# Another table of issue places for the delta rule's steps on TensorE, VectorE and ScalarE

## The reference

```python
S = S * gt[..., None]
pred = jnp.einsum('bhk,bhkv->bhv', kt, S)
delta = (vt - pred) * bt[..., None]
S = S + kt[..., None] * delta[:, :, None, :]
o = jnp.einsum('bhk,bhkv->bhv', qt, S)
```

## Time and profile before

| what | value |
| --- | --- |
| runs | 1614.93, 1616.38, 1616.94 us; median 1616.38 |
| the profiled execution's own time | 1616.59 us |
| its span, first to last instruction | 1614.8 us |
| mean granted TensorE clock | 0.964 |
| busy: TensorE, VectorE, ScalarE | 1409.9, 1199.5, 1019.0 us |
| ScalarE's instructions | 2716 |

### The profile page before, as it was taken

One profiled execution on the slowest core, in us unless ns is written; L12 is line 12 of the kernel. 1 busy time (PEld: TensorE's weight loads), 2 busy tenths in 40 slices (PEclk: granted clock), 3 DMA queues, 4 the chain that ended last, 5 costly groups with the idle time before them and its releaser, 6 DMA issues. The chain is left out here.

```text
span 1614.8 us, 41750 instructions
## 1 busy us (share of the span) xinstructions
PE 1409.9 (87%) x15104; PEld 937.5 (58%) x15104; DVE 1199.5 (74%) x3775; ACT 1019.0 (63%) x2716; POOL 41.2 (3%) x49
## 2 busy tenths in 40 slices
PE   6888889978999878888988989988989889988888
PEld 2544555656455446556756756665666667566634
DVE  6848888974842487898888889898888988974221
ACT  5617888995611456777777777686777767754220
POOL 0000000000000000000000000000000000000000
PEclk9989899989999997999999999999999999979999
DMA  4025001000030011122121212212121211200010
GB/s 168 0 83 128 15 15 28 2 2 1 1 134 0 28 31 49 20 62 56 23 66 52 69 20 63 61 31 52 58 63 19 69 55 23 51 25 15 0 55 26
DMA packets 128489, 69.30 MB, mean 43 GB/s; under 512 B 104464, under 2 KB 115984, under 8 KB 127264
## 3 DMA queue, kind: packets, MB, share of 16 engines
q1 hardware_dynamic: 128288, 66.64, 15.3%
HBM read 51.36 MB, written 6.98 MB: 36 GB/s over the span
## 5 line engine op out<-in xcount | busy, mean ns | idle before, releaser
L1666 DVE SCALAR_TENSOR_TENSOR arena<-arena 128x1024 f32<-128x1024 f32 x144 | 183.0, 1280 | 19.6 <-ACT arena L1235 19.3
L882 PE MATMUL bank<-xt,arena 128*128 128x512 f32 x384 | 183.1, 608 | 9.6 <-ACT arena L1227 8.2
L1745 DVE TENSOR_TENSOR arena<-arena 128x512 f32<-128x512 f32 x224 | 155.2, 693 | 9.5 <-PE bank L938 4.5
L716 PE MATMUL bank<-xt,arena 128*128 128x512 f32 x320 | 142.2, 601 | 3.8 <-DVE arena L1478 3.8
L1234 ACT COPY arena<-bank 128x512 f32<-128x512 f32 x96 | 56.2, 585 | 92.4 <-PE bank L882 90.8
L882 PEld LDWEIGHTS bank<-xt,arena 128*128 128x128 f32 x384 | 68.4, 194 | 71.9 <-issue 71.6
L716 PEld LDWEIGHTS bank<-xt,arena 128*128 128x128 f32 x320 | 60.3, 192 | 85.3 <-issue 85.1
L735 PE MATMUL bank<-arena 128*128 128x256 f32 (+2 forms) x384 | 98.4, 404 | 6.2 <-DVE arena L1478 5.3
L938 PEld LDWEIGHTS bank<-arena 128*32 128x32 f32 x5120 | 59.8, 115 | 75.5 <-issue 64.4
L1164 ACT ACTIVATE arena<-arena 128x128 f32<-128x128 f32 x256 | 99.5, 393 | 0.0
L938 PE MATMUL bank<-arena 128*32 128x32 f32 x5120 | 74.7, 204 | 25.8 <-DVE arena L1747 17.3
(11 more groups left out here) (170 smaller groups left out, 3313.3 us busy)
## 6 DMA issues: line engine op xcount, KB each, us to landing
arena<-d_w SPq DMA_DIRECT2D x16, 519.0 KB, 6.4
arena<-beta_scratch SPq DMA_DIRECT2D x16, 512.0 KB, 5.7
arena<-zero_scratch SPq DMA_DIRECT2D x14, 512.0 KB, 4.6
arena<-arena SPq DMA_DIRECT2D x64, 64.0 KB, 2.6
arena<-zero_scratch SPq DMA_DIRECT2D x15, 256.0 KB, 2.9
arena<-arena SPq DMA_DIRECT2D x12, 256.0 KB, 3.8
arena<-w_scratch SPq DMA_DIRECT2D x2, 1376.0 KB, 6.1
arena<-f_idx SPq DMA_DIRECT2D x2, 1072.0 KB, 8.4
```

Of the source, the lines that this page charges most:

```text
L716: last = pe.matmul(bank[2 * w + n % 2][0:rows, :], (WU if f < 2 else WU1R)[:, w, k, m * P:m * P + rows], XT[:, k, hf * HALF:(hf + 1) * HAL ...
L882: last = pe.matmul(bank[b][:], DW[:, par, c:c + P], XT[:, k, rhs], start=(k == 0), stop=(k == KC - 1))
L1666: dve.scalar_tensor_tensor(out=CT[:, x], in0=RAW[:, x, 3 - j:3 - j + S], scalar=DW[:, par, tap:tap + 1], in1=CT[:, x], op0=ALU.mult, op1=A ...
L1745: dve.tensor_tensor(kq, kq, left, ALU.mult)
```

## The change

It replaces the numbers of the three tables `"pe"`, `"act"` and `"dve"` of `PLACE`. The steps are the same, and so is all other code. Many numbers move without changing the order. In the diff, a step's neighbours tell whether it did.

```diff
--- before.py
+++ after.py
@@ -61,56 +61,56 @@
 
 PLACE = {
     "pe": [
-        (0.226, "piece", 7), (0.432, "piece", 2), (0.486, "piece", 3), (0.582, "piece", 1), (0.596, "piece", 0),
-        (0.692, "piece", 6), (0.733, "piece", 4), (0.774, "piece", 5), (0.966, "norm", 0), (0.993, "norm", 1),
-        (1.267, "level", 0, 1), (1.281, "level", 0, 0), (1.322, "turn_v", 1), (1.363, "level", 1, 1), (1.39, "level", 1, 0),
-        (1.445, "level", 2, 1), (1.459, "level", 2, 0), (1.5, "level", 3, 1), (1.514, "level", 3, 0), (1.541, "norm_q"),
-        (1.555, "level", 4, 0), (1.637, "level", 5, 0), (1.664, "turn_v", 0), (1.705, "level", 4, 1), (1.842, "level", 5, 1),
-        (1.856, "level", 6, 0), (1.884, "gate", 0), (1.938, "level", 6, 1), (1.952, "gate", 1), (2.021, "left", 4, 0),
-        (2.034, "left", 4, 1), (2.062, "right", 4, 0), (2.116, "right", 4, 1), (2.13, "left", 5, 0), (2.144, "left", 5, 1),
-        (2.185, "right", 5, 0), (2.212, "keys", 0), (2.24, "right", 5, 1), (2.253, "left", 6, 0), (2.295, "right", 6, 0),
-        (2.308, "left", 6, 1), (2.336, "keys", 1), (2.349, "solve", 0), (2.377, "right", 6, 1), (2.404, "update", 0),
-        (2.473, "predict", 1), (2.527, "solve", 1), (2.568, "update", 1), (2.61, "predict", 2), (2.623, "solve", 2),
-        (2.651, "update", 2), (2.719, "predict", 3), (2.747, "solve", 3), (2.76, "update", 3), (2.788, "predict", 4),
-        (2.801, "solve", 4), (2.829, "update", 4), (2.87, "predict", 5), (2.897, "solve", 5), (2.925, "update", 5),
-        (2.979, "predict", 6), (3.007, "solve", 6), (3.048, "update", 6), (3.075, "predict", 7), (3.103, "solve", 7),
-        (3.158, "update", 7), (3.199, "final"), (3.418, "turn_out", 0), (3.678, "turn_out", 1), (3.815, "project", 0),
-        (3.911, "project", 1), (4.089, "project", 2), (4.171, "project", 3),
+        (0.212, "piece", 7), (0.445, "piece", 2), (0.486, "piece", 3), (0.568, "piece", 1), (0.61, "piece", 0),
+        (0.692, "piece", 6), (0.747, "piece", 4), (0.788, "piece", 5), (0.979, "norm", 0), (1.007, "norm", 1),
+        (1.281, "level", 0, 1), (1.295, "level", 0, 0), (1.336, "turn_v", 1), (1.377, "level", 1, 1), (1.404, "level", 1, 0),
+        (1.459, "level", 2, 1), (1.473, "level", 2, 0), (1.514, "level", 3, 1), (1.527, "level", 3, 0), (1.555, "norm_q"),
+        (1.582, "level", 4, 0), (1.651, "level", 5, 0), (1.678, "turn_v", 0), (1.719, "level", 4, 1), (1.856, "level", 5, 1),
+        (1.87, "level", 6, 0), (1.897, "gate", 0), (1.938, "level", 6, 1), (1.966, "gate", 1), (2.034, "left", 4, 0),
+        (2.062, "left", 4, 1), (2.075, "right", 4, 0), (2.13, "right", 4, 1), (2.144, "left", 5, 0), (2.158, "left", 5, 1),
+        (2.199, "right", 5, 0), (2.24, "left", 6, 0), (2.253, "right", 5, 1), (2.267, "keys", 0), (2.308, "right", 6, 0),
+        (2.322, "left", 6, 1), (2.349, "solve", 0), (2.363, "keys", 1), (2.39, "right", 6, 1), (2.418, "update", 0),
+        (2.5, "predict", 1), (2.541, "solve", 1), (2.596, "update", 1), (2.623, "predict", 2), (2.637, "solve", 2),
+        (2.664, "update", 2), (2.733, "predict", 3), (2.76, "solve", 3), (2.774, "update", 3), (2.801, "predict", 4),
+        (2.815, "solve", 4), (2.842, "update", 4), (2.884, "predict", 5), (2.925, "solve", 5), (2.952, "update", 5),
+        (2.993, "predict", 6), (3.021, "solve", 6), (3.048, "update", 6), (3.089, "predict", 7), (3.116, "solve", 7),
+        (3.171, "update", 7), (3.226, "final"), (3.432, "turn_out", 0), (3.705, "turn_out", 1), (3.829, "project", 0),
+        (3.911, "project", 1), (4.103, "project", 2), (4.185, "project", 3),
     ],
     "act": [
-        (0.412, "piece", 7), (0.465, "piece", 2), (0.482, "piece", 3), (0.518, "piece", 1), (0.553, "piece", 0),
-        (0.623, "silu", 1), (0.675, "piece", 6), (0.693, "exp_z"), (0.763, "square", 1), (0.781, "piece", 4),
-        (0.816, "piece", 5), (0.868, "ln_z"), (1.061, "norm", 0), (1.079, "norm", 1), (1.096, "exp_k"), (1.132, "exp_g"),
-        (1.202, "silu", 2), (1.237, "silu", 0), (1.289, "square", 0), (1.36, "turn_v", 1), (1.605, "level", 5, 0),
-        (1.64, "turn_v", 0), (1.728, "flip"), (1.851, "level", 5, 1), (1.904, "gate", 0), (1.921, "level", 6, 0),
-        (1.956, "level", 6, 1), (1.974, "gate", 1), (2.009, "left", 4, 0), (2.026, "left", 4, 1), (2.149, "left", 5, 1),
-        (2.167, "left", 5, 0), (2.254, "keys", 0), (2.272, "left", 6, 0), (2.307, "right", 6, 0), (2.325, "left", 6, 1),
-        (2.377, "solve", 0), (2.395, "keys", 1), (2.43, "update", 0), (2.5, "solve", 1), (2.535, "update", 1),
-        (2.57, "solve", 2), (2.588, "right", 6, 1), (2.658, "update", 2), (2.711, "solve", 3), (2.746, "update", 3),
-        (2.798, "solve", 4), (2.833, "update", 4), (2.886, "solve", 5), (2.939, "update", 5), (2.991, "solve", 6),
-        (3.044, "update", 6), (3.114, "solve", 7), (3.184, "update", 7), (3.219, "final"), (3.342, "rows", 0),
-        (3.447, "rows", 1),
+        (0.412, "piece", 7), (0.447, "piece", 2), (0.5, "piece", 3), (0.535, "piece", 1), (0.553, "piece", 0),
+        (0.64, "silu", 1), (0.658, "piece", 6), (0.675, "exp_z"), (0.763, "square", 1), (0.781, "piece", 4),
+        (0.816, "piece", 5), (0.851, "ln_z"), (1.044, "norm", 0), (1.079, "norm", 1), (1.114, "exp_k"), (1.132, "exp_g"),
+        (1.202, "silu", 2), (1.237, "silu", 0), (1.289, "square", 0), (1.36, "turn_v", 1), (1.623, "turn_v", 0),
+        (1.711, "level", 5, 0), (1.746, "flip"), (1.868, "level", 5, 1), (1.904, "gate", 0), (1.939, "gate", 1),
+        (1.956, "level", 6, 0), (1.991, "level", 6, 1), (2.009, "left", 4, 0), (2.061, "left", 4, 1), (2.149, "left", 5, 1),
+        (2.167, "left", 5, 0), (2.254, "left", 6, 0), (2.272, "keys", 0), (2.307, "right", 6, 0), (2.325, "left", 6, 1),
+        (2.377, "solve", 0), (2.395, "keys", 1), (2.43, "update", 0), (2.482, "solve", 1), (2.518, "update", 1),
+        (2.57, "right", 6, 1), (2.588, "solve", 2), (2.605, "update", 2), (2.693, "solve", 3), (2.728, "update", 3),
+        (2.798, "solve", 4), (2.833, "update", 4), (2.886, "solve", 5), (2.921, "update", 5), (2.974, "solve", 6),
+        (3.026, "update", 6), (3.096, "solve", 7), (3.184, "update", 7), (3.219, "final"), (3.342, "rows", 0),
+        (3.465, "rows", 1),
     ],
     "dve": [
-        (0.483, "conv", 1, 0), (0.541, "conv", 1, 1), (0.576, "conv", 1, 2), (0.866, "conv", 0, 0), (0.913, "conv", 2, 0),
-        (0.983, "soft"), (0.994, "conv", 2, 1), (1.017, "conv", 2, 2), (1.029, "conv", 0, 1), (1.076, "conv", 0, 2),
-        (1.134, "key", 0), (1.157, "total", 0), (1.169, "key", 1), (1.203, "key", 2), (1.215, "total", 1),
-        (1.25, "level", 0, 1), (1.262, "total", 2), (1.273, "advance", 0, 1), (1.285, "advance", 0, 0),
-        (1.297, "level", 0, 0), (1.308, "advance", 1, 1), (1.32, "advance", 1, 0), (1.331, "level", 1, 1),
-        (1.355, "level", 1, 0), (1.378, "level", 2, 1), (1.39, "level", 2, 0), (1.401, "advance", 2, 1),
-        (1.413, "advance", 2, 0), (1.436, "level", 3, 1), (1.448, "level", 3, 0), (1.459, "total", 3),
-        (1.471, "advance", 3, 0), (1.494, "norm_q"), (1.506, "advance", 4, 0), (1.517, "advance", 3, 1),
-        (1.552, "level", 4, 0), (1.587, "invert"), (1.599, "less", 1), (1.61, "less", 2), (1.622, "less", 3),
-        (1.634, "less", 4), (1.645, "less", 5), (1.669, "less", 6), (1.68, "less", 7), (1.692, "less", 8), (1.715, "less", 9),
-        (1.727, "less", 10), (1.738, "less", 11), (1.75, "less", 12), (1.762, "less", 13), (1.773, "less", 14),
-        (1.808, "level", 4, 1), (1.82, "advance", 4, 1), (1.843, "total", 4), (1.855, "advance", 5, 0), (1.878, "total", 5),
-        (1.936, "advance", 5, 1), (1.948, "advance", 6, 0), (2.052, "right", 4, 0), (2.087, "advance", 6, 1),
-        (2.099, "total", 6), (2.122, "right", 4, 1), (2.192, "right", 5, 0), (2.238, "right", 5, 1), (2.366, "update", 0),
-        (2.424, "predict", 1), (2.529, "update", 1), (2.564, "predict", 2), (2.657, "update", 2), (2.703, "predict", 3),
-        (2.785, "update", 3), (2.831, "predict", 4), (2.901, "update", 4), (2.924, "predict", 5), (2.959, "update", 5),
-        (3.006, "predict", 6), (3.041, "update", 6), (3.064, "predict", 7), (3.145, "update", 7), (3.227, "stats"),
-        (3.343, "turn_out", 0), (3.797, "turn_out", 1), (3.89, "project", 0), (3.971, "project", 1), (4.11, "project", 2),
-        (4.18, "project", 3),
+        (0.529, "conv", 1, 0), (0.564, "conv", 1, 1), (0.599, "conv", 1, 2), (0.89, "conv", 0, 0), (0.924, "conv", 2, 0),
+        (1.017, "conv", 2, 1), (1.041, "conv", 2, 2), (1.052, "soft"), (1.076, "conv", 0, 1), (1.122, "conv", 0, 2),
+        (1.157, "key", 0), (1.18, "total", 0), (1.192, "key", 1), (1.227, "key", 2), (1.262, "total", 1),
+        (1.273, "level", 0, 1), (1.285, "total", 2), (1.297, "level", 0, 0), (1.308, "advance", 0, 1),
+        (1.32, "advance", 0, 0), (1.331, "total", 3), (1.343, "advance", 1, 1), (1.366, "level", 1, 1),
```

(14 more changed lines are left out.)

## The result

The new table takes 1627.79 us (median of 20 runs, 1608.88 to 1640.52), the old one in the same session 1616.46 (20 runs, 1608.22 to 1622.42): ratio 1.0040, 95% interval 1.0021 to 1.0060. It is **slower**, by 11 us in the medians, where 1614.2 was forecast.

The account below looks back on a forecast made before the run. TensorE and VectorE both busy, neither full, with 12.3 us of TensorE idle per pair; odd windows -0.35, even +0.1, seven each, plus head 9's half microsecond: about -2.2 us, so 1614.2, range 1604 to 1625.

Parts of the forecast that it names:

- even windows hang on left 4 0 and left 4 0 on flip: TensorE's left 4 0 starts when the last x part lands, in transfers released by ScalarE's flip 14.6 us before.
- piece 1's wait: TensorE: piece 1 waits about 1 us for bank 1, emptied by piece 3's copy on ScalarE.
- level 4 0's and piece 4's waits gone: TensorE: level 4 0 no longer waits for L1747, and piece 4's wait of 0.47 us goes.
- the flip costs in full: Slower rival, chance 0.24: ScalarE's flip 1.0 us late, each even window 0.6 longer, odd ones gain nothing; 1620.6 us.
- Flip ... it is 0.5 late: ScalarE: flip behind level 5 0 and update 3 comes 0.5 us late; even windows end 0.1 later.
- piece 1 ahead of level 4 0 ... gain 0.1: TensorE: piece 1 fills the 1.13 us gap before level 4 0, leaving a 1.0 gap; gain 0.1 us.
- a loss of 1.1: Lower bound for piece 1's move: its bank's copy is late once more and level 4 0 delays advance 4 0.
- conv 2 1, conv 2 2 ... and the totals ... nothing, bounds 0.2 either way: These steps change places in stretches with microseconds to their readers: no effect, bounds 0.2 us either way.
- The sign to look for: If right, the wait before left 4 0 in even windows grows by about 0.5 us, flip standing behind update 3.
- Level 5 0 later ... carried on: 0.47: ScalarE: level 5 0 later frees piece 6 earlier; TensorE's piece 4 through predict 4 move up 0.47 us, bounds 0 and 0.8.
- 0.35 shorter: Summed forecast for each odd window: -0.35 us, seven of them in the kernel.
- such a stretch at 1.2 GHz can come or go: Granted clock as an addition to the range: one window at 0.95 takes about 4 us more than its like.

Follow-up runs that it names:

- e5: Old table with TensorE's level 4 0 moved behind piece 1 (and update 1): 1626.56 us for the old table's 1619.26, ratio 1.0060.
- e9: Old table with the new table's VectorE queue, TensorE's and ScalarE's queues unchanged: ratio 1.0022 to the old table.
- e6: Old table with ScalarE's level 5 0 moved behind flip, ahead of update 3: ratio 1.0015 to the old table.
- e0: The new table once more, unchanged, for a second profile: 1630.92 us, ratio 1.0095 to the old table.
- e8: New table with 6 products of identity matrices ahead of left 4 0's wait in even heads from 2 on: ratio 0.9979 to the old table.
- e17: New table with 6 identity products ahead of left 4 0's wait in even heads, run again in another session: ratio 0.9974 to the old table.
- e16: New table with TensorE's level 4 0 put back ahead of piece 1, flip staying late: ratio 1.0068 to the old table.
- e15: New table with 6 identity products behind, not ahead of, left 4 0's wait in even heads: ratio 1.0065 to the old table.

## Why the prediction was wrong

*Right:* that even windows hang on left 4 0 and left 4 0 on flip; piece 1's wait (0.94 for 1.0); level 4 0's and piece 4's waits gone; and the rival "the flip costs in full" named the right place and sign.

*"Flip ... it is 0.5 late" failed.* It is 1.24 late in head 10, 0.85 by the median of the even heads. The sum took less 14 and invert as unmoved; they are 0.86 and 0.62 later. Two steps can make them so. One is "piece 1 ahead of level 4 0 ... gain 0.1": I priced TensorE's gap and not who waits for level 4 0 on VectorE, though the lower bound, a loss of 1.1, named just that. e5 shows 5.5 to 7.3 us for it in the old table (with update 1 ahead of level 4 0 too); in the new one no run shows its price apart. The other is "conv 2 1, conv 2 2 ... and the totals ... nothing, bounds 0.2 either way": VectorE's moves alone make invert 0.8 late (e9). Which of them does was not taken apart. The sign to look for was off by its own terms as well: flip 0.5 late and a middle 0.47 faster make the wait at left 4 0 grow by 1.0, not by the 0.5 stated. It grew by 1.4 by the medians.

*"Level 5 0 later ... carried on: 0.47" failed.* The gap at piece 4 went, but piece 4 itself starts no earlier: predict 3 ahead of it waits for VectorE's update 2. I followed the gap, not the start. In the old table the term held (e6, odd windows); in the new one (e0's trace) odd windows are 0.3 longer (58.2 for 57.9 us), not 0.35 shorter.

*The clock was only in the range.* This is the largest miss. I wrote that "such a stretch at 1.2 GHz can come or go", as chance. It was put at nothing in the sum, and it hung on the very wait that the change lengthens: filled, the wait costs nothing and the clock is held, and the table's whole loss is gone (e8, e17). Of e0's 16.2 us some 8 are clock by the 127 runs. By six pairs the order's share is small: e17, whose order is the new one, is under before, though at a better clock. How much is left for the order, 0 to 3 us, the runs don't settle: filled, it shows none; in e0's trace even windows without a fall take 54.7 us for 54.5 and odd ones 58.2 for 57.9 (medians of heads 4 to 12), 0.5 more in a pair, 3 in six. With those 3 and the 6.5 us of L938's waits taken off, the four falls within after's six pairs cost (19.6 - 9.5) / 4 = 2.5 us each; with the waits left in, 4.2; and e16's four, with its rest of 3.0 off, (15.6 - 3.0) / 4 = 3.2. In e0's trace the two even windows with a fall (58.75 and 58.42 us) are 3.9 longer than those without, their own longer waits included. These are estimates: some 2 to 4 us a fall.

The price of the rival, 1620.6, had flip 1.0 late, near what came, and was 7 us short because the clock was not in it either. 1627.8 lay outside of the range, 2.8 over its end.

## What to carry to other kernels

Price a wait on TensorE twice: once as time, and once as the clock of what stands behind it; a wait of 2 us in front of 10 us of small matmuls cost, by estimate, 2 to 4 us more than itself. When a step moves back on one engine, look at everything queued behind its reader on the other, before counting the gap that is filled. If a wait can't be had out of the way, fill it with products that end when it does, and no longer.

## What the runs showed of the hardware

- The granted clock was still 1.00 in the wait of 1.94 us itself and for 0.8 us behind it; it fell once TensorE worked again, and stayed low through 10.2 us of which the engine was busy for 9.93. In e15, with large matmuls behind a wait of 2.31 us, it was low for little more than their 2.90 us, and at 1.00 again in the small ones that followed.
- The wait's length alone doesn't say whether it falls: in e0's trace waits of 2.17 and 1.72 us (heads 2 and 4) passed at 1.00, in the new table's first trace 2.28 and 2.06 at the same heads did not. The mean clock goes with much of the spread of a kernel's runs: within a session it accounts for 81% of the variance of the 127 runs of the old table.
- The old table's median moved between sessions from 1614.8 to 1620.4 us, along with its mean clock, 0.965 to 0.961: as much as half of this change. The sessions ran on different chips, and the two on the same chip agree (1619.3 and 1619.3), so this can be the chip. The same new table stood at 1.0040 in one session and 1.0095 in another, and these intervals don't overlap. So a ratio is safest beside others of its own session.
